# A deformable-conv block on one core: the fusion conv by the F(2,3) minimal filter along the rows, blends made in the gather slots

## What is computed

```python
out_normal = _conv(x, w_normal)                    # 3x3, 128 -> 128
offset = jnp.concatenate([_conv(x, w_offx), _conv(x, w_offy)], axis=1)   # 18 channels
out_x = _deform_conv(x, offset, w_dx)              # 9 taps, each sampled bilinearly at pixel + tap + offset
out_y = _deform_conv(x, offset, w_dy)              # the same samples, other weights
out = _conv(jnp.concatenate([out_normal, out_x, out_y], axis=1), w_fusion)   # 3x3, 384 -> 128
out = jax.nn.relu(_bn(out, bn1_g, bn1_b, bn1_m, bn1_v))
out = _bn(_conv(out, w_conv2), bn2_g, bn2_b, bn2_m, bn2_v)                   # 3x3, 128 -> 128
return jax.nn.relu(out + x)
```

## Time and profile before

| | us |
|---|---|
| median of 3 runs | 2706.47 (2705.27 to 2708.77) |
| the profiled execution, its own time | 2705.52 |
| its span, first to last instruction | 2703.7 |

### The profile page before, as it was taken

One profiled execution on the slowest core, in us unless ns is written; L12 is line 12 of the kernel. 1 busy time (PEld: TensorE's weight loads), 2 busy tenths in 40 slices (PEclk: granted clock), 3 DMA queues, 4 the chain that ended last, 5 costly groups with the idle time before them and its releaser, 6 DMA issues.

```text
span 2703.7 us, 51420 instructions
## 1 busy us (share of the span) xinstructions
PE 2606.2 (96%) x17840; PEld 2598.1 (96%) x17840; DVE 1845.7 (68%) x4940; ACT 2001.4 (74%) x4925; POOL 1881.7 (70%) x1806
## 2 busy tenths in 40 slices
PE   3679999999999999999999999999999999999999
PEld 3679999999999999999999999999999999999999
DVE  5777776766676777777767776776766776777730
ACT  5678787777777777777777777777777777777741
POOL 6777777767777676777777776777767777676720
PEclk7789999999999999999999999999999999999999
DMA  5766766767666676666666666666666666666620
GB/s 170 219 203 198 213 205 205 205 189 209 197 205 199 201 206 205 200 200 204 199 203 200 203 198 201 200 200 197 200 194 206 200 205 200 203 207 195 194 76 20
DMA packets 162404, 522.70 MB, mean 193 GB/s; under 512 B 30944, under 2 KB 31072, under 8 KB 161760
## 3 DMA queue, kind: packets, MB, share of 16 engines
q0 software_dynamic: 144000, 471.97, 59.9%
q1 hardware_dynamic: 18144, 47.44, 5.1%
HBM read 506.18 MB, written 13.11 MB: 192 GB/s over the span
## 4 chain that ended last, share of the span: by engine, by line
PE 91%; DVE 2%; ACT 2%; DMA 2%; issue 1%; POOL 1%; ACTq 0%; POOLq 0%; DVEq 0%
PE work L340 19%; PE work L346 19%; PE work L343 19%; PE acc L343 7%; PE acc L340 7%; PE acc L346 7%; PE turned L372 7%; PE work L325 4%; DMA cells<-in_cells,index 2%; POOL cells L299 1%; DVE mixed L677 1%; ACT mixed L472 1%; PE work L332 1%; ACT samp L472 1%; DVE samp L683 0%
## 5 line engine op out<-in xcount | busy, mean ns | idle before, releaser
L299 POOL DMA_INDIRECT cells<-in_cells,index x1800 | 1870.4, 1039 | 705.1 <-issue 342.2
L472 ACT ACTIVATE mixed<-cells,wgt 128x256 f32<-128x256 f32 x1800 | 761.4, 499 | 51.2 <-DMA cells<-in_cells,index 50.4
L472 ACT ACTIVATE samp<-mixed,wgt 128x128 f32<-128x128 f32 x1800 | 620.5, 395 | 205.8 <-DVE mixed L677 197.2
L677 DVE SCALAR_TENSOR_TENSOR mixed<-cells,wgt,mixed 128x256 f32<-128x256 f32 x1800 | 745.9, 477 | 35.0 <-ACT mixed L472 33.4
L340 PE MATMUL work<-feat,w_hi 128*128 128x320 f32 x2160 | 691.4, 320 | 1.4 <-ACT off_c L471 1.4
L346 PE MATMUL work<-feat,w_lo 128*128 128x320 f32 x2160 | 676.0, 313 | 0.0
L343 PE MATMUL work<-feat,w_hi 128*128 128x320 f32 x2160 | 675.7, 313 | 0.0
L683 DVE SCALAR_TENSOR_TENSOR samp<-mixed,wgt,samp 128x128 f32<-128x128 f32 x1800 | 512.5, 345 | 59.5 <-ACT samp L472 59.5
L636 DVE TENSOR_TENSOR samp_lo<-turned,samp_hi 128x640 fp32r<-128x640 f32 x360 | 294.5, 818 | 273.8 <-ACT samp_hi L471 273.8
L340 PE MATMUL acc<-samp_hi,w_hi 128*128 128x320 f32 x1440 | 448.8, 312 | 0.0
L343 PE MATMUL acc<-samp_lo,w_hi 128*128 128x320 f32 x1440 | 447.6, 311 | 0.0
(11 more groups left out here) (70 smaller groups left out, 3180.7 us busy)
## 6 DMA issues: line engine op xcount, KB each, us to landing
cells<-in_cells,index POOLq DMA_INDIRECT x1800, 3.7
x_raw<-in_xflat SPq DMA_DIRECT2D x40, 410.0 KB, 4.2
late<-in_x SPq DMA_DIRECT2D x40, 320.0 KB, 5.3
out<-late SPq DMA_DIRECT2D x40, 320.0 KB, 3.7
late<-in_weights SPq DMA_DIRECT2D x3, 1152.0 KB, 7.4
cells<-in_weights SPq DMA_DIRECT2D x1, 657.0 KB, 4.0
cst<-in_const SPq DMA_DIRECT2D x1, 199.0 KB, 4.6
bnp<-in_bn SPq DMA_DIRECT2D x1, 4.0 KB, 4.9
```

The source lines that it names most:

```text
L299: eng.indirect_dma_start(out=cells[:, g, :], out_offset=None, in_=table[0:(b + 1) * CELLS, :], in_offset=bass.IndirectOffsetOnAxis(ap=inde ...
L472: return eng.activation(dst, src, ACT.Copy, scale=scale)
L677: eng.scalar_tensor_tensor(out=mixed[:, tp, j], in0=cells[:, (k * TILES + j) % GSLOTS, 2 * C:4 * C], scalar=wgt[:, par, 1, 0, j, k:k + 1], ...
```

## The change

The fusion conv is made by the F(2,3) minimal filter along the rows. For a pair of output rows t, t+1 and a column tap, with input rows d0 to d3 and the three row taps g0, g1, g2, it uses four products in place of six:

- part 0: (d1 + d2) by (g0 + g1 + g2)/2; part 1: (d2 - d1) by (g0 - g1 + g2)/2; part 2: (d0 - d2) by g0; part 3: (d1 - d3) by g2.
- row t is product 0 + product 1 + product 2; row t+1 is product 0 - product 1 - product 3.

A part is 9 groups (3 channel groups by 3 column taps) of three matmuls, each 320 columns (4 row pairs by 80). In detail:

- TensorE: `SLICES` gives F four entries of 9 groups (slots 3 to 6) in place of two of 27 over slots 2 to 7. The fusion conv has 108 matmuls a strip, before 162. One table holds for all steps.
- VectorE makes the row sums: in slots 0, 1, 2 and 4, `part_add` adds or subtracts rows of `feat` (now 3 planes of plain float32) into `part_sum`, 128x960, before the tap's blends; `part_high` copies it rounded to `part_hi`, and `part_low` writes the rest to `part_lo`, after `samples_low`. Three slots of parts turn.
- The output sums: ScalarE copies product 0 out in slot 3; VectorE makes its sum and difference with product 1 (slot 4), adds product 2 (slot 5), subtracts product 3 (slot 6). Then ScalarE does one ReLU and one rounded copy of 640 elements, and VectorE one subtraction of 640, in slot 6.
- `feat` holds no high and low parts any more: VectorE's subtractions for `acc` (4 of 320) and for the normal conv (2 of 320) are gone, ScalarE copies `acc` with 2 instructions of 640 in place of 4 of 320, and its edge-row copies are half as long.
- The blends are made in place: `upper` writes to the slot of `cells`, the first blend writes there too, and the second reads from it. `mixed` is gone. GpSimd's gather waits for the second blend (`samp_done`) where it waited for the first (`mixed_done`).
- Weights come in seven loads of 9 x 128 elements; the four that were late come in steps 0 and 1. VectorE and ScalarE make the transformed taps (`weights_sum`, `weights_high`, `weights_low`). `dynamic_dma_scratch_size` is 8192 in place of the default 16384.

The diff, cut to its core:

```diff
+SLICES = [
+    [("C", 0, 0, 9)],
+    [("O", 0, 0, 3), ("O", 1, 0, 3), ("C", 1, 0, 3)],
+    [("C", 1, 3, 9)],
+    [("F", 0, 0, 9)],
+    [("F", 1, 0, 9)],
+    [("F", 2, 0, 9)],
+    [("F", 3, 0, 9)],
+    [("N", 0, 0, 9)],
     [("N", 1, 0, 9)],
 ]
-GROUPS = {"O": 3, "F": 27, "N": 9, "C": 9}
-
-FIRST_SLICES = [
-    [("O", 0, 0, 3), ("O", 1, 0, 3)],
-    [("F", 0, 0, 7)],
-    [("F", 0, 7, 16)],
-    [("F", 0, 16, 25)],
-    [("F", 0, 25, 27), ("F", 1, 0, 7)],
-    [("F", 1, 7, 16)],
-    [("F", 1, 16, 25)],
-    [("F", 1, 25, 27), ("N", 0, 0, 7)],
-    [("N", 0, 7, 9), ("N", 1, 0, 9)],
-]
-FIRST_STEPS = 4
-WEIGHTS_AT = {1: {7: 2}, 2: {1: 3}}
-
-
-def done(slices):
-
-    return [[(j, h) for j, h, a, b in s if b == GROUPS[j]] for s in slices]
+LENGTH = {"O": 3, "F": 9, "N": 9, "C": 9}
...
+INDEX_AT = 3
+PART_AT = {0: 0, 1: 1, 2: 2, 4: 3}
+PART_SLOTS = 3
+WEIGHTS_AT = {0: {2: 3, 5: 4}, 1: {2: 5, 5: 6}}
...
-        feat = sb("feat", [128, 2, 6, SLOT_ROWS, PITCH], F32R)
+        feat = sb("feat", [128, 2, GROUPS_IN, SLOT_ROWS, PITCH])
+        part_hi = sb("part_hi", [128, PART_SLOTS, GROUPS_IN, HR, PITCH], F32R)
+        part_lo = sb("part_lo", [128, PART_SLOTS, GROUPS_IN, HR, PITCH], F32R)
+        part_sum = sb("part_sum", [128, GROUPS_IN * HALF])
+        fused = sb("fused", [128, HALF + PIX])
+        prod1 = fused[:, 0:HALF].rearrange("p (t w) -> p t w", w=W)
+        pre = fused[:, HALF:HALF + PIX].rearrange("p (t q w) -> p t q w", q=2, w=W)
...
-                    at_least(eng, mixed_done, PER * c + q - GSLOTS + 1)
+                    at_least(eng, samp_done, PER * c + q - GSLOTS + 1)
...
                     if job == "F":
-                        hi, lo, base = feat[:, par, 2 * g, rows, cols], feat[:, par, 2 * g + 1, rows, cols], FUSE
+                        slot = (PARTS * s + part) % PART_SLOTS
+                        hi, lo = part_hi[:, slot, n // 3, :, cols], part_lo[:, slot, n // 3, :, cols]
+                        base = FUSE + 9 * part
...
+                        if job == "F":
...
+                            at_least(eng, part_lo_done, PARTS * s + part + 1)
...
+                    copy(cells[:, g, 0:2 * C], cells[:, g, 0:2 * C], scale=wgt[:, par, 0, 0, j, k:k + 1])\
                         .then_inc(upper_done, 1)
...
+                    if k == 3 and fl.fuse:
+                        at_least(eng, f_done, PARTS * s + 1)
+                        at_least(eng, pre_half, s)
+                        copy(fused[:, 0:HALF], work[BANK["F", 0]][:, 0:HALF]).then_inc(prod1_out, 1)
...
+                    if k == 6 and fl.fuse:
+                        at_least(eng, pre_done, 2 * s + 2)
+                        eng.activation(fused[:, HALF:HALF + PIX], fused[:, HALF:HALF + PIX], ACT.Relu, bias=scale1[:, 1:2],
+                                       scale=scale1[:, 0:1]).then_inc(f_out, 1)
+                        at_least(eng, f_out, s + 1)
+                        at_least(eng, c_done, 2 * (s - 2) + 2)
+                        copy(mid[:, par, 0, 1:1 + ROWS, 1:1 + W],
+                             fused[:, HALF:HALF + PIX].rearrange("p (r w) -> p r w", w=W)).then_inc(mid_hi_done, 1)
...
-                        for half in range(2):
-                            rows = slice(1 + half * HR, 1 + half * HR + HR)
-                            copy(feat[:, par, 2 + 2 * d, rows, 1:1 + W],
-                                 acc[2 * d + half][:, 0:HALF].rearrange("p (r w) -> p r w", w=W)).then_inc(acc_hi_done, 1)
+                        copy(feat[:, par, 1 + d, 1:1 + ROWS, 1:1 + W].rearrange("p (h r) w -> p h r w", h=2),
+                             acc[d][:, :, 0:HALF].rearrange("p h (r w) -> p h r w", w=W)).then_inc(acc_out, 1)
...
-                        out=mixed[:, tp, j], in0=cells[:, (k * TILES + j) % GSLOTS, 2 * C:4 * C],
-                        scalar=wgt[:, par, 1, 0, j, k:k + 1], in1=mixed[:, tp, j], op0=ALU.mult, op1=ALU.add,
+                        out=cells[:, g, 0:2 * C], in0=cells[:, g, 2 * C:4 * C],
+                        scalar=wgt[:, par, 1, 0, j, k:k + 1], in1=cells[:, g, 0:2 * C], op0=ALU.mult, op1=ALU.add,
...
+            def part_add(s, part):
+
+                q = PARTS * s + part
+                first, other, op = ((1, 2, ALU.add), (2, 1, ALU.subtract), (0, 2, ALU.subtract), (1, 3, ALU.subtract))[part]
+                at_least(eng, acc_out, 2 * s + 2)
+                at_least(eng, n_out, 2 * s + 2)
+                if part == 2:
+                    at_least(eng, top_done, s)
+                if part == 3:
+                    at_least(eng, bot_done, s + 1)
+                at_least(eng, part_lo_done, q)
+                rows = feat[:, s % 2]
+                eng.tensor_tensor(part_sum[:].rearrange("p (g t w) -> p g t w", g=GROUPS_IN, w=W),
+                                  rows[:, :, first:first + 7:2, 1:1 + W], rows[:, :, other:other + 7:2, 1:1 + W],
+                                  op).then_inc(part_summed, 1)
+
+            def part_high(s, part):
+                q = PARTS * s + part
+                at_least(eng, part_summed, q + 1)
+                at_least(eng, f_done, q - PART_SLOTS + 1)
+                at_least(eng, zeroed, 4)
+                eng.tensor_copy(part_hi[:, q % PART_SLOTS, :, :, 1:1 + W],
+                                part_sum[:].rearrange("p (g t w) -> p g t w", g=GROUPS_IN, w=W)).then_inc(part_hi_done, 1)
+
+            def part_low(s, part):
+                q = PARTS * s + part
+                at_least(eng, part_hi_done, q + 1)
+                low(part_lo[:, q % PART_SLOTS, :, :, 1:1 + W],
+                    part_sum[:].rearrange("p (g t w) -> p g t w", g=GROUPS_IN, w=W),
+                    part_hi[:, q % PART_SLOTS, :, :, 1:1 + W]).then_inc(part_lo_done, 1)
...
+                    if fl.fuse and k in PART_AT:
+                        part_add(s, PART_AT[k])
...
+                        part_high(s, PART_AT[k])
+                        part_low(s, PART_AT[k])
...
+                    if fl.fuse and k == 4:
+                        prod2 = work[BANK["F", 1]][:, 0:HALF].rearrange("p (t w) -> p t w", w=W)
+                        at_least(eng, f_done, PARTS * s + 2)
+                        at_least(eng, prod1_out, s + 1)
+                        at_least(eng, mid_hi_done, s)
+                        at_least(eng, mid_lo_done, s)
+                        eng.tensor_tensor(pre[:, :, 0], prod1, prod2, ALU.add)
+                        eng.tensor_tensor(pre[:, :, 1], prod1, prod2, ALU.subtract).then_inc(pre_half, 1)
+                    if fl.fuse and k == 5:
+                        prod0 = work[BANK["F", 2]][:, 0:HALF].rearrange("p (t w) -> p t w", w=W)
+                        at_least(eng, f_done, PARTS * s + 3)
+                        at_least(eng, pre_half, s + 1)
+                        eng.tensor_tensor(pre[:, :, 0], pre[:, :, 0], prod0, ALU.add).then_inc(pre_done, 1)
+                    if fl.fuse and k == 6:
+                        prod3 = work[BANK["F", 3]][:, 0:HALF].rearrange("p (t w) -> p t w", w=W)
+                        at_least(eng, f_done, PARTS * s + 4)
+                        eng.tensor_tensor(pre[:, :, 1], pre[:, :, 1], prod3, ALU.subtract).then_inc(pre_done, 1)
+                        at_least(eng, mid_hi_done, s + 1)
+                        low(mid[:, par, 1, 1:1 + ROWS, 1:1 + W],
+                            fused[:, HALF:HALF + PIX].rearrange("p (r w) -> p r w", w=W),
+                            mid[:, par, 0, 1:1 + ROWS, 1:1 + W]).then_inc(mid_lo_done, 1)
```

More of the change, by code:

```diff
@@ L95, with __init__ @@
 class Flags:
[L98 to L115 removed]
+    def __init__(self, i):
+        self.strip = i < NS
+        self.nxt = i + 1 < NS
+        self.load = i + 2 < NS
+        self.top = 1 <= i < NS
+        self.bot = 1 <= i <= NS
+        self.fuse = 2 <= i < NS + 2
+        self.mtop = 3 <= i < NS + 2
+        self.mbot = 3 <= i <= NS + 2
+        self.resid = 3 <= i < NS + 3
+        self.second = 4 <= i < NS + 4
+        self.weights = WEIGHTS_AT.get(i, {})
     def has(self, job):
@@ L126, in at_least @@
 def at_least(eng, sem, value):
[L128 removed]
+    if value <= 0:
         return
@@ L318, in wcol, with take @@
                 return slice((base + n) * C, (base + n + 1) * C)
+            freed = [None, None]
+            def take(b):
+                if freed[b] is not None:
+                    eng.wait_ge(*freed[b])
             def offsets(par, half):
+                dst = work[BANK["O", half]]
                 for n in range(9):
@@ new lines, in step @@
+                        upper(T + 3, i + 1, k + 3 - TAPS, 1 - par)
+                    if fl.second and k in (0, 2):
+                        half = k // 2
+                        at_least(eng, c_out, 2 * (i - 4) + half + 1)
+                        part = resid[:, par, half * HALF:(half + 1) * HALF]
+                        eng.activation(part, part, ACT.Relu, bias=scale1[:, 3:4]).then_inc(out_ready, 1)
+                    if k == 1 and fl.nxt:
```

(14 more changed lines are left out.)

397 lines of the change are left out of this document (175 added, 222 removed), and 8 rows, old and new, of the table SLICES.

## The result

The changed kernel takes **2830.34 us** (median of 4 runs, 2827.84 to 2835.16), the kernel before 2705.87 on the same chip: a ratio of **1.046** (95% interval 1.0442 to 1.0479). The forecast was 2731 us and slower, with 2650 to 2810 as its range: the sign holds, and 99 us are missing from the sum.

The account below looks back on a forecast made before the run. TensorE bounds the kernel at 64.5 us a strip, GpSimd next at 61.4. The terms 24.4, 187, 37 x (61.4 + 4.0) = 2420, 22 and 75 span 2728, forecast as 2731 us, +0.9%; range 2650 to 2810.

Parts of the forecast that it names:

- part 1: TensorE, fusion conv: 54 matmuls fewer a strip, -8.1 us; TensorE then needs 56.4 us, under GpSimd's 61.4.
- The clock rival: TensorE loses its clock to gaps; at 0.85 it needs 66.4 us a strip, 2768 us in all; chance 0.05.
- the base: GpSimd's gathers as the bound, before the holds that the change adds: 61.4 us a strip.
- part 3: Gathers held at their start by VectorE's added instructions: +3.3 us a strip by additions, +0.8 by copies, +4.0 taken.
- Part 2: VectorE's added row sums, copies and output sums: 56.9 us a strip and some 2 of waits, under GpSimd's 61.4.
- The rival in which VectorE becomes the bound: Copies of 1.16 us and waits make gathers wait for second blends: 68 us a strip, 2827 us; chance 0.07.
- The model of a random meeting: Gathers start every 1.25 us and meet an addition's first 1.02 us by chance: mean hold 0.51, so 0.42 us each.
- Gathers slip past: Gathers keep in step with VectorE, so the eight additions hold few: +1 us a strip, 2620 us; chance 0.28.
- The copies hold for their whole length: VectorE's rounding copies hold gathers throughout: +2 us a strip, 2805 us; chance 0.08.
- Part 4: GpSimd's gather waits for a tile's second blend, one run of five later: 0, bounds 0 and 1 us a strip.
- the sign that I had put down for VectorE as the bound: GpSimd's waits on second blends of over 2 us.
- Parts 5 to 7: ScalarE's work 0; first three strips 187 us; end 22 us to the last tap, then 75 of convs.

Follow-up runs that it names:

- e8: Kernel before with 18 of the 27 groups in each half of the fusion conv, 54 matmuls fewer a strip, nothing added: 2611.99 us, ratio 0.9648.
- e2: Changed kernel with the second half of the second conv wholly in slot 2, not split over slots 1 and 2: 2713.03 us, ratio 1.0028.
- e11: e5 with each rounding copy of the row sums made twice: 2760.22 us, ratio 1.0208.
- e12: e5 with each row sum and each remainder made in three instructions of 320 elements: 2705.62 us, ratio 1.0005.
- e5: e2 with `samples_low` between VectorE's two runs of blends and ScalarE making its input earlier: 2675.82 us, ratio 0.9885.
- e7: e2 with each row sum and each remainder made in three instructions of 320 elements: 2760.02 us, ratio 1.02.
- e14: e12 with `x_low` moved from slot 8 to behind the second blends of the next step's slot 0: 2679.06 us, ratio 0.9899.
- e15: e11 with `x_low` moved from slot 8 to behind the second blends of the next step's slot 0: 2720.39 us, ratio 1.0059.
- e10: Changed kernel with the order of e5 alone, the second conv's half still split between slots 1 and 2: 2817.08 us, ratio 1.0423.

## Why the prediction was right and wrong

**The bound now, and part 1.** GpSimd was the second bound, 3 us under the first: right, and its strip nearly, at 62.4 for 61.4 (e8), 37 us too low over the run. The 54 matmuls went. That TensorE then needs 56.4 us a strip was low: it is busy 59.9 (1754.58/29.3), at a granted clock of 0.95. The clock rival had the mechanism and put 0.85. In the timeline above TensorE stands still from 927.2 to 931.59; the two stretches that follow (the columns of the earlier trace rows) are at its two levels, 1.2 and 2.4 GHz.

```profile
931.59:936.00 4.41, 4.41 (x16) 4.41 (x17) 4.13 (x11) 3.18 (x8) 1.99 (x3) 0.50 0.50 153
936.60:941.00 4.40, 4.40 (x35) 4.38 (x35) 2.48 (x4) 2.70 (x6) 3.25 (x4) 1.00 0.64 172
```

All 29 waits for `off_c` between 521.06 and 2450 us are followed by some 6 us of matmuls at the lower level, and only three of the 56 waits of transposes for `samp_lo` are (the one at 922.21 is one of them). Half of those 6 us, by my estimate, is most of the 3.5 us a strip over the forecast. In e2 the clock is 0.98. So the lost clock came with the wait of slot 1; how much of e2's 117 us is the wait itself and how much the clock behind it, no run separates.

**The step that failed** is the one that isn't there. Part 1 counted what `SLICES` removes and never what it puts next to what. The new table queues three groups of the second conv behind the offsets in slot 1, on the offsets' bank; for a queue with a wait added I should have named what stands behind it. It had no term and no rival; its size is e2's 117 us (3.7 us a strip), against a forecast miss of 99. Without it, 2731 would have been within 18 us of e2's 2713, and part of that nearness is luck: the base was 1.0 us a strip too low (62.4 for 61.4) and part 3 was 2.0 too high.

**Part 2.** Right: the additions take 1.154 and 1.159 us for 1.16; the copy 0.651 for 0.7. The estimate of 0.66 by the rule for a copy of this kind in the Trainium skill (VectorE: DVE Perf Modes, What auto-detection actually checks) agrees better still. VectorE is busy 55.5 us of a steady strip (1625.36/29.3) for 56.9. But I gave its waits 2 us, and they are 12 (341.7 us of named waits in 28.3 strips). The rival in which VectorE becomes the bound came to the right time (2827) with the wrong cause: its copies of 1.16 us don't exist. Its half on the waits was the better half, and e11 and e12 show how near this bound lies.

**Part 3.** Held per strip: 9.2 forecast (5.2 + 4.0), 9.4 measured, and the agreement is luck. The eight additions hold 2.4 us for 3.3, the copies 0.4 for 0.8, and the blends, which I left alone, 6.3. With GpSimd as the bound, the change adds 2.0 (e8's 6.2 to e2's 8.2), half of the +4.0 that was to decide the sum: gathers that start in row sums, remainders and copies hold 2.8 in e2, and those that start in blends 4.7 for 6.0 in e8. The holds past five further instructions had no place in the model, though the kernel before has nine of them in the same gathers (0.7 us a strip). The copy's "half-second-long" is half a microsecond. The model of a random meeting fails in kind: gathers start in step with VectorE (in slot after slot of e5 one starts 0.39 us into a remainder and takes 1.59), so that shortening an instruction moves the meeting rather than shortens it (e7, e14). *Gathers slip past* was wrong: it put the additions at +1 us, and they hold 2.4 in the changed kernel and 3.1 in e5, whose order lowers the holds in blends (4.7 to 4.2, from e2). *The copies hold for their whole length* was wrong by e15.

**Part 4.** The later slot rule costs nothing where GpSimd is the bound (0.1 in e5). In the changed kernel GpSimd waits 2.05 us a strip for second blends beyond its fixed 0.303, the sign that I had put down for VectorE as the bound; in e2, with slot 1 repaired, it is 0.1. No run takes back the blends in the slots, the seven weight loads or the smaller scratch by itself; e2 has all three, and GpSimd's waits there are 0.2 in all.

**Parts 5 to 7.** The work of ScalarE was rightly costed at nothing; its place in the queue was not. The first three strips took 188.9 us for 187. From the last gather to the last tap 20 us for 22, and then 83 for 75. These two ends give 8 of the missing us, and 37 strips at 67.8 in place of 65.4 the other 90.

**The ledger.** 37 x (67.8 - 65.4) = 90; start 2; end 6; span 2826.2 for 2728.

## What to carry to other kernels

When a schedule is rewritten, read it as queues: for each instruction that takes a PSUM bank or a slot, ask which engine must empty it, how late that copy stands in its own queue, and what is waiting behind the taker. Work saved on the bound engine is worth at most the distance to the next bound (93 us here, by e8), and a fix for that next bound shows little until the waits ahead of it are gone (13 us in e10, 37 from e2 to e5). A sum of busy and waiting time near 100% says nothing of an in-order engine; add work to it and see if the waits absorb it.

## What the runs showed of the hardware

- A gather's issue is held when it starts in a VectorE instruction with two SBUF inputs or in a 128x960 fp32r copy, until 0.12 to 0.14 us before its end: 0.31 us at 0.21 us into a copy of 0.65, 0.65 at 0.39 into a remainder of 1.16. A gather that is under way when such a copy starts takes 1.09 us for 0.95 (e15, 901.90).
- A gather that starts in a run of such instructions can be held to the end of the run: 2.05 us across seven blends. At nearly the same phase of a run (1.21 us in, both 952.07 and e5's 889.34) it was held once and once not at all. What decides that was not found.
- Two-input instructions split in three hold less by themselves for the most part (e2 to e7: the remainders 1.57 to 0.25 us a strip, the row sums 0.87 to 1.00; e5 to e12: both together 3.1 to 0.7). In all it is as much as before in e7 (8.2) and less in e12 (6.3 for 7.7).
- TensorE's granted clock was 0.50 for some 6 us of matmuls behind each of the 29 waits of 4.4 to 5.6 us for `off_c`, and 1.00 after them (16 matmuls in 4.41 us, then 35 in 4.40).
